# Weighted row tiles summed on VectorE before one fold on TensorE, corner weights in PSUM, and moved convolutions and copies

## The reference

```python
    x = x + _L0_conv_ref(_gn(x), L0_conv_weight, L0_conv_bias)
    x = x + _L1_conv_ref(_gn(x), L1_conv_offset_w, L1_conv_offset_b, L1_conv_prelu_a, L1_conv_dconv_w, L1_conv_dconv_b)
    x = x + _L2_conv_ref(_gn(x), L2_conv_conv_w, L2_conv_ds_w, L2_conv_bn_gamma, L2_conv_bn_beta, L2_conv_bn_mean, L2_conv_bn_var)
    x = x + _L3_conv_ref(_gn(x), L3_conv_W_conv, L3_conv_b_conv, L3_conv_W_edge, L3_conv_W_att1, L3_conv_b_att1, L3_conv_W_att2, L3_conv_b_att2)
    return x
```

```python
            corners = [(y0, x0, (y0 + 1 - py) * (x0 + 1 - px)), (y0, x0 + 1, (y0 + 1 - py) * (px - x0)), (y0 + 1, x0, (py - y0) * (x0 + 1 - px)), (y0 + 1, x0 + 1, (py - y0) * (px - x0))]
            y = jnp.einsum('bgikhw,goik->bgohw', s, wg).reshape(B, Cout, H, W)
```

## Time and profile before

| | us |
|---|---|
| median of 3 runs (lowest, highest) | 4552.56 (4544.15, 4554.67) |
| the profiled execution's own time | 4534.8 |
| its span, first to last instruction | 4533.0 |
| TensorE busy | 4221.4 (93%) |
| GpSimd busy | 3256.4 (72%) |
| VectorE busy | 2922.9 (64%) |
| ScalarE busy | 1808.1 (40%) |

### The profile page before, as it was taken

How to read it: one execution, slowest core, us unless ns; L and a number is a source line. 1 busy time by engine, 2 the same in 40 slices (tenths; PEclk the granted TensorE clock), 3 DMA queues, 4 the chain that set the end, 5 groups by cost and what they waited for, 6 DMA issues and landing times.

```text
span 4533.0 us, 74261 instructions
## 1 busy us (share of the span) xinstructions
PE 4221.4 (93%) x24997; PEld 2019.7 (45%) x24997; DVE 2922.9 (64%) x5468; ACT 1808.1 (40%) x1991; POOL 3256.4 (72%) x3094
## 2 busy tenths in 40 slices
PE   2799999999999999999999999999999999999992
PEld 2344444444444444444444444444444444444440
DVE  4556667666766666666667766766676666667552
ACT  1334344334443444444344444443444444444431
POOL 1777777777777777777777777777777777777750
PEclk9899999999999999999999999999999999999995
DMA  3677787877778787777868877787777878778752
GB/s 101 205 226 236 225 247 219 243 227 235 238 233 241 227 251 239 234 241 225 245 218 246 247 229 241 222 247 234 236 239 233 241 226 241 241 230 249 235 184 63
DMA packets 479569, 1024.32 MB, mean 226 GB/s; under 512 B 261924, under 2 KB 298116, under 8 KB 474628
## 3 DMA queue, kind: packets, MB, share of 16 engines
q1 hardware_dynamic: 325636, 516.15, 39.3%
q10 hardware_dynamic: 55296, 302.01, 19.6%
q0 software_dynamic: 98304, 201.52, 15.7%
HBM read 864.66 MB, written 73.99 MB: 207 GB/s over the span
## 4 chain that ended last, share of the span: by engine, by line
PE 68%; DMA 8%; DVE 8%; SPq 5%; POOL 5%; issue 5%; ACT 1%; ACTq 0%; DVEq 0%; POOLq 0%
PE ps_r L1454 48%; POOL ring L600 5%; PE ps_y L1466 5%; PE ps_c L1440 5%; DMA taps_c<-plane_act 4%; PE ps_a L1393 3%; SPq L414 3%; DMA wino<-xn_a 2%; PE ps_t L1480 2%; DMA plane_act<-act_c 2%; DVE ring L1177 1%; DVE col_hat L1166 1%; PE ps_a L1440 1%; PE ps_y L1487 1%; SPq L420 1%
## 5 line engine op out<-in xcount | busy, mean ns | idle before, releaser
L600 POOL DMA_INDIRECT ring<-patch_table,idx_part x3072 | 3248.2, 1057 | 1126.2 <-issue 1114.0
L1454 PE MATMUL ps_r<-select,image 128*128 128x512 f32 x6912 | 3170.2, 604 | 54.4 <-ACT image L661 49.3
L1454 PEld LDWEIGHTS ps_r<-select,image 128*128 128x128 f32 x6912 | 1262.5, 191 | 1452.8 <-issue 1432.8
L1166 DVE TENSOR_TENSOR col_hat<-ps_r,col_hat 128x512 f32<-128x512 f32 x1152 | 794.4, 690 | 1381.1 <-PE ps_r L1454 1339.8
L650 ACT ACTIVATE select<-row_in,minus_row 128x1536 f32<-128x1536 f32 x384 | 605.0, 1575 | 788.3 <-PE ps_r L1454 730.1
L652 ACT ACTIVATE select<-select,one_col 128x1536 f32<-128x1536 f32 x384 | 605.4, 1577 | 12.5
L1177 DVE TENSOR_TENSOR ring<-ring,w_cur 128x768 f32<-128x768 f32 x512 | 486.4, 950 | 20.1 <-DMA ring<-patch_table,idx_part 20.1
L669 ACT COPY samples<-ps_t 128x512 f32<-128x512 f32 x256 | 149.8, 585 | 849.8 <-PE ps_t L1480 849.8
L1466 PEld LDWEIGHTS ps_y<-col_hat,w_dense 128*32 128x32 f32 x9216 | 229.0, 110 | 298.0 <-issue 297.9
L1466 PE MATMUL ps_y<-col_hat,w_dense 128*32 128x128 f32 x9216 | 332.2, 277 | 0.0
L1181 DVE TENSOR_TENSOR ring<-ring 128x384 f32<-128x384 f32 x512 | 282.3, 551 | 4.4
(11 more groups left out here) (230 smaller groups left out, 2300.9 us busy)
## 6 DMA issues: line engine op xcount, KB each, us to landing
row_in<-coord_table ACTq DMA_DIRECT2D x384, 768.0 KB
col_hat<-coord_table SPq DMA_DIRECT2D x384, 768.0 KB
ring<-patch_table,idx_part POOLq DMA_INDIRECT x3072
taps_c<-plane_act SPq DMA_DIRECT2D x144, 268.1 KB
taps_c<-xn_c SPq DMA_DIRECT2D x192, 130.0 KB
coord_table<-wino SPq DMA_DIRECT2D x64, 216.0 KB
wino<-xn_a SPq DMA_DIRECT2D x96, 130.0 KB
plane_act<-act_c SPq DMA_DIRECT2D x192, 65.0 KB
```

The costliest lines, as they stand in the source:

```text
L600: nc.gpsimd.indirect_dma_start(out=ring[j][:, h % 2, k, :], out_offset=None, in_=table, in_offset=bass.IndirectOffsetOnAxis(ap=idx_part[:, ...
L1166: v.tensor_tensor(hat_t, ps_r[:, (s + t) % 2], hat_t, ALU.mult).then_inc(tile_weighed, 1)
L1454: ins = mm(ps_r[:, (s + t) % 2], image[:, m, t], select[s % 2][:, m], start=(m == 0), stop=(m == PAIRS - 1))
```

## The change

- `sum_tiles` on VectorE: after tile 2 of a slot is weighed, tile 1 is added to tile 0 in place; in the next slot, after its tile 0 is weighed, tile 2 of the slot before is added. tiles_summed counts the second addition. `fold_dense` waits for it and folds the sum once (8 instructions); dense_folded counts slots.
- ps_t becomes the second bank of ps_c. The freed bank, ps_w, holds the weights of one part (`take_weights`) and the weighed lower two corners (`lower`); `weigh_corners` is two instructions of 384 columns.
- New waits for the shared bank: LAST_READ before some turns, `second_bank` before the second half of some convolutions.
- The absolute value and the minimum on the column distances move from VectorE to ScalarE (slot 21), with a changed sign that w_dense loses too.
- ScalarE places image tiles 0 and 1 in slot 23 of the period before.
- TensorE: the offset convolution at (14, 2) instead of (14, 1), `a` ahead of `c` in a third, the edge convolution's two halves ahead of the wait for edges.
- Head: table clearing after the weight loads, `prepare_rest` of VectorE at the start of slot 23 of period -1, tap copies shared by two queues. Tail: tap copies shared, and for the last image direct copies in place of the path over DRAM.

```diff
+LAST_READ = {8: "downb", 11: "conv1b", 14: "conv2b", 17: "conv3b", 23: "excite"}
...
-        ps_t = psum("ps_t", [P, HALF])
+        ps_w = psum("ps_w", [P, HALF])
+        ps_t = ps_c[:, 1]
...
+        lower = ps_w[:, 0:GTAPS * 2 * C].rearrange("p (k f) -> p k f", f=2 * C)
+        w_part = ps_w[:, GTAPS * 2 * C:GTAPS * 2 * C + JB * GTAPS * CORNERS].rearrange("p (j k m) -> p j k m", j=JB, k=GTAPS)
...
-            def copy_taps(dst, src, done):
+            def copy_taps(dst, src, done, shared):
+                for to, frm in copies(dst, src, range(0, SHIFTS * STRIPS, 2 if shared else 1)):
+                    sp.dma_start(to, frm).then_inc(done, 16)
...
-            sp.dma_start(table.rearrange("(p q) f -> p q f", p=P),
-                         zeros[:, None, :].to_broadcast([P, 2 * BLOCKS, PATCH])).then_inc(table_cleared, 16)
...
-                if s == 2 and known_zero(n):
+                if s == 0 and known_zero(n):
                     load_later()
+                    sp.dma_start(table.rearrange("(p q) f -> p q f", p=P),
+                                 zeros[:, None, :].to_broadcast([P, 2 * BLOCKS, PATCH])).then_inc(table_cleared, 16)
...
+                    if last_image(n):
+                        copy_taps(taps_act, act_c, taps_act_in, True)
+                    else:
+                        store_plane(plane_act, act_c, plane_out)
...
+                if s == 21:
+                    act.wait_ge(a_dve.sem, a_dve.at(n, "columns"))
+                    cols = coords_t[:, 2 * PAIRS:]
+                    chain.step(nc.scalar.activation(cols, cols, ACT.Abs))
+                    nc.scalar.activation(cols, cols, ACT.Relu, bias=one_col[0:DSEL], scale=-1.0).then_inc(a_act.sem, 1)
...
-                    place_image(n)
+                    place_image(n, (2,))
...
                 if e == DT - 1 and live(n):
-                    for k in range(CHUNKS):
-                        turn(n, g, k)
+                    turn(n, g, 0)
+                if s == SLOTS - 1 and live(n + 1):
+                    place_image(n + 1, (0, 1))
+                if e == DT - 1 and live(n):
+                    turn(n, g, 1)
...
+                if first_image(n + 1):
+                    a_copies(n + 1, s)
+                if last_image(n - 1):
+                    c_copies(n - 1, s)
...
+            def sum_tiles(n, s, t):
+                hats = col_hat[s % 3]
+                if t == 1:
+                    dve.wait_ge(tile_weighed, (n * SLOTS + s) * WT + 2)
+                    tiles_added[0] = chain.add(v.tensor_tensor(hats[:, 0], hats[:, 0], hats[:, 1], ALU.add))
+                else:
+                    dve.wait_ge(tile_weighed, (n * SLOTS + s) * WT + WT)
+                    if s < SLOTS - 1:
+                        chain.upto(tiles_added[0])
+                    v.tensor_tensor(hats[:, 0], hats[:, 0], hats[:, 2], ALU.add).then_inc(tiles_summed, 1)
...
-                return chain.add(v.tensor_tensor(tile, tile, wts, ALU.mult))
+                chain.add(v.tensor_tensor(lower.rearrange("p k (m c) -> p k m c", c=C), corners[:, :, 2:],
+                                          by_corner[:, :, 2:], ALU.mult))
+                return chain.add(v.tensor_tensor(corners[:, :, 0:2], corners[:, :, 0:2], by_corner[:, :, 0:2], ALU.mult))
...
+                return chain.add(v.tensor_copy(w_part, w_cur[:].rearrange("p (j g) k m -> p g j k m", g=PARTS)[:, g]))
...
                 for q in range(WT):
                     if live(n):
                         weigh_tile(n, s, q)
+                    before = (n, s - 1) if s > 0 else (n - 1, SLOTS - 1)
+                    if q == 0 and live(before[0]):
+                        sum_tiles(*before, 2)
+                    if q == WT - 1 and live(n):
+                        sum_tiles(n, s, 1)
...
-                if at == (14, 1):
+                if at == (14, 2):
...
-                for t in range(WT):
-                    pe.wait_ge(tile_weighed, (n * SLOTS + s) * WT + t + 1)
-                    for j in range(JB):
-                        ins = mm(ps_y[j * C:(j + 1) * C, :],
-                                 w_dense[:, DT - 1 - e].rearrange("p g o -> p (g o)"),
-                                 col_hat[s % 3][:, t, j * P:(j + 1) * P], start=(e == 0 and t == 0), stop=False)
-                    ins.then_inc(dense_folded, 1)
+                pe.wait_ge(tiles_summed, n * SLOTS + s + 1)
+                for j in range(JB):
+                    ins = mm(ps_y[j * C:(j + 1) * C, :], w_dense[:, DT - 1 - e].rearrange("p g o -> p (g o)"),
+                             col_hat[s % 3][:, 0, j * P:(j + 1) * P], start=(e == 0), stop=False)
+                ins.then_inc(dense_folded, 1)
...
+            def second_bank(n, s):
+                if live(n + 1):
+                    pe.wait_ge(copied, ((n + 1) * PARTS + s // DT) * CHUNKS + CHUNKS)
...
                         if e == DT - 1 and q != 1:
+                            if q == 0 and s in LAST_READ and live(n - 1):
+                                pe.wait_ge(c_act.sem, c_act.at(n - 1, LAST_READ[s]))
                             turn(n, g, q // 2)
+                    if live(n + 1):
+                        a(n + 1, s, q)
                     if live(n - 1):
                         c(n - 1, s, q)
-                    if live(n + 1):
-                        a(n + 1, s, q)
```

104 lines of the change are left out of this document (64 added, 40 removed).

## The result

The changed kernel takes 5225.9 us (median of 4 runs, 5222.4 to 5234.55) against 4553.61 before (4 runs): a ratio of 1.1507, with an interval of 1.1486 to 1.1527. The forecast was 5090, with a range to 5335: slower, and by 540 us where 672 came. The profiled execution took 5223.52 us, with a span of 5221.7 against 4533.0: 688.7 us more to account for. The mean granted clock of TensorE is 0.942, against 0.974.

A forecast was written before the change was run, and what follows sets the result against it. TensorE, busy 4156 of 4274 us, was taken as the bound. On the profiled execution -169 + 557 + 248 - 70 - 24 - 22 - 14 + 34 = +540 us, giving a forecast of 5090 us, range 4790 to 5335.

The forecast's parts named there:

- The new wait: Before each fold, TensorE stands through one VectorE weighing and one addition: at least 1.45 us in 384 slots, +557 us.
- VectorE's lateness: Where VectorE is still at other work when the row tile ends, the stall before the fold grows: +248 us.
- rival 1: VectorE catches up everywhere in its idle time, leaving 1.45 us stalls and no clock loss: 4811 us, chance 12%.
- The folds: TensorE's fold_dense falls from 24 to 8 matmul instructions a slot: -169 us.
- The clock: Stalls drop TensorE's clock to 1.2 GHz, one drop an image at 2.1 us: +34 us, upper end 272.
- rival 2: TensorE's clock drops after each of five long stalls an image: 5331 us, chance 12%.
- the forecast case: Whole kernel: all terms as priced give 5090 us, own range 4900 to 5260, chance 67%.
- The image boundary: Between images, earlier ScalarE copies remove TensorE's 49.3 us of waiting and 21 us of clock loss: -70 us.
- The taps' waits: Convolutions on TensorE: reordering them removes part of the waits for taps, -24 us (0 to -60).
- PSUM bank shared: Transposes and convolution copies wait for the shared bank's earlier readings, done in time: nothing; 38 us without that cover.
- corner weighing in PSUM: VectorE's two 384-column multiplications replace one of 768; nothing added for a PSUM operand.
- Head and tail: Start and end of the kernel get shorter by rearranged clearing, preparation and copies: head -22 us, tail -14 us.

The follow-up runs named there:

- sum_first: Changed kernel with VectorE adding the last tile of the slot before ahead of weighing tile 0 of this slot: 4826.38 us, ratio 1.0613.
- filler1: Changed kernel plus one needless row product a slot on TensorE between the first row tile and the fold: 5114.21 us, ratio 1.124.
- filler2: Changed kernel plus two needless row products a slot on TensorE between the first row tile and the fold: 5088.43 us, ratio 1.1199.
- image_early: Kernel before the change, with only ScalarE's image tiles 0 and 1 placed in slot 23 of the period before: 4530.84 us, ratio 0.9995.
- no_sum: Changed kernel without the two additions, the three folds of 8 instructions put back, all else kept: 4525.08 us, ratio 0.9967.
- one_add_sbuf: Changed kernel with only tile 1 added to tile 0, 16 fold matmuls, and the old SBUF corner weighing put back: 4500.24 us, ratio 0.9896.
- one_add_early: Changed kernel with only tile 1 added to tile 0, in the second third of a slot, and 16 fold matmuls: 4504.73 us, ratio 0.992.
- one_add: Changed kernel with only tile 1 added to tile 0, in the last third; TensorE folds that sum and tile 2 (16 matmuls): 4469.72 us, ratio 0.9852.
- sum_early: Changed kernel with each addition right behind its tile's weighing, in the second and last thirds of the slot: 4518.18 us, ratio 0.9961.

## Why the prediction was right, and where it wasn't

**The new wait and VectorE's lateness: right.** The forecast had 557 + 248 = 805 us, the waits show 772.3. At 1.38 us each for the floor (530) that leaves 242 for lateness, against 248. The floor rested on the order in the code and three rows, the lateness on replaying one image third by third with the added work. The replay had 11 of 24 slots late; the trace has 10 or 11 stalls of over 1.6 us in every image but the last, which has 5. Five an image were to reach 2.9 us; 62 of the 384 do, four an image. The idle time that VectorE had in sum (rival 1) was no help, as it lay in other thirds. `sum_first` shows both parts apart from each other: it removes the floor in the slots that are early, and leaves 394 us of waits in the rest. My expectation for that run, which had the lateness go as well, was wrong, by forgetting that the sum would still stand behind the third's work.

**The folds: right.** -158 us against -169.

**The clock: right in mechanism, mis-sized, and the largest miss.** The term was +34 us, one drop an image at 2.1 us, because the shortest wait with a drop behind it in the earlier trace rows was 2.91 us. The trace shows 104 more stretches at 1.2 GHz and 186 us of loss, 1.8 us each. The price of one was good, the count was not: 6.5 more an image, instead of one. I had looked at three image boundaries only. In the changed kernel drops follow waits of 2.0 us too, and the kernel before had drops after waits of 2.2 to 2.7 us elsewhere that I had not looked for. None of the 232 waits of under 1.75 us in the changed kernel had a drop behind it, and 122 of the 159 waits of 1.9 us or more had one; but in `sum_first` drops came behind waits of 1.41 us. The upper end of this term, 272, held it, and with it the range. By the mechanism this lies nearer to rival 2 (five long stalls an image, each with a drop) than to the forecast case; the Trainium skill's page "TensorE: Matmul & The Clock Gate", section "HAM oscillation", spoke for it. The trace agrees with it, with 122 drops in the changed kernel; and `filler1` and `filler2` bring the clock back by work alone.

**The image boundary: wrong.** The step "two of three image copies move into slot 23: the 49.3 us of waiting go", with its 21 us of clock, gave -70. `image_early` has 0, with an interval from -10 to +5 us. The copies were the last releaser that the trace could name, but the turn of TensorE's own loop was there underneath: 2.73 us at one boundary with the copies long done, 41.3 of 45.2 us over the 13 turns. In the changed kernel 13 to 16 us went (54.4 to 41.2 by the group's idle time, 53.2 to 36.9 by the gaps of over 0.3 us).

**The taps' waits: gone, but not for the reason given, and not in the size.** I had -24 for the reordered convolutions. In the changed kernel all 44 us of gaps before convolutions that wait for taps went, and 19 us before the edge sums and the norms' sums, 64 in all. In `no_sum`, where TensorE runs at full pace with the same order, 66 us of gaps before the convolutions are there. So the waits went because the stalls gave the transfers time, not by the reordering, which by itself brought no gain.

**PSUM bank shared, corner weighing in PSUM, both put at nothing: right**, as no wait of TensorE for ScalarE's copies out of PSUM shows up, and the three instructions of 384 columns take 546 to 556 ns with one operand in PSUM against 551 without. The additions of tiles take 0.683 us against 0.684.

**Head and tail: right.** -19 against -22, and -9.5 against -14: the tail is 106.7 us long, where about 102 was forecast.

Together: the two steps that were wrong and the clock nearly account for the difference, +152 for the clock, +54 for the boundary, -40 for the taps and the other waits, -33 for the wait, +11 for the folds, +8 for head and tail: +152 in all against the +149 by which the span (5222) exceeds the 5073 of the forecast. That the number is off by no more than the clock is luck in part, as the other errors, up to 54 us each, cancel. The last row tile ended at 5115.0, not near 4970, TensorE's share is 81%, the mean stall 2.01 us.

**The rest of the change** is worth -21 us by `no_sum`, all of it in the head and the tail. In the middle, its relief of GpSimd (1.057 to 1.001 us a gather) brings no time: the middle of `no_sum` is 18 us longer. Once TensorE's work falls it may count: with the weighing in SBUF, `one_add_sbuf`, GpSimd is full, but a gain in time isn't shown clear of noise.

What stays open: why `no_sum` has 26 stretches at 1.2 GHz where the kernel before has 18 (the 18 us more of clock loss are as much as its middle is longer); what besides its length decides whether a stall drops the clock; whether `one_add_early` is slower than `one_add`; and what the weighing through PSUM is worth in time.

## What to carry to other kernels

Before work is moved from the full engine to one with idle time, look at when the result will be wanted and what stands ahead of it on the engine that gets it: here 262 + 262 us of additions on an engine idle for a third of the time cost 701 us in one place and, with the folds they save, nothing in another, and half the move was worth more than the whole (4470 us against 4518 on the same chip). Replay one period with the new work, third by third, and price each stall twice: its length, and the low clock behind it, for which all waits of the trace are to be looked through and not the three that come to hand. Even so the count stays uncertain, as the same stall length had a drop behind it in one kernel and none in another. And a wait that a trace puts down to one releaser may have a second floor beneath it; where the same gap comes once a loop turn, suspect the turn.

## What the runs showed of the hardware

- A turn of the loop held TensorE for 2.5 to 3.5 us between its matmuls in the changed kernel, 3.2 to 4.0 in `no_sum` and 2.0 to 3.7 in `image_early`, with every input ready. It stands in the trace under "issue", or under a semaphore that came beside it.
- The granted clock fell to 1.2 GHz behind waits as short as 1.94 us in the changed kernel and 1.41 us in `sum_first`, in a TensorE that was busy before and after. Here is the clock behind one of them, the wait of 2.01 us before 2306.77 in the changed kernel (one of 2.88 us had ended 5 us earlier), in windows right behind it and later:

```profile
2306.80:2308.20 1.40, 1.40 (x25) 1.02 (x25) 1.11 (x3) 1.09 (x2) 0.00 (x0) 0.53 0.46 179
...
2311.60:2315.00 3.40, 3.40 (x10) 1.49 (x9) 2.76 (x6) 0.34 (x1) 2.49 (x4) 1.00 0.81 302
```

- Needless matmuls in a stall made a kernel faster, by 112 and 137 us.
- A gather on GpSimd took 1.001 us in the mean in the changed kernel and in `no_sum`, both with VectorE's corner work through PSUM; 1.015 to 1.032 in the kernels with that corner work, one or two additions a slot and few stalls (`one_add`, `one_add_early`, `sum_early`); 1.057 with the corner work in SBUF, and 1.085 with an addition beside it.
- A PSUM operand made a VectorE multiplication or addition of 384 columns no slower: 546 to 556 ns, against 551 (kernel before) and 556 (`one_add_sbuf`) from SBUF alone.
